# Half tiles, 64 side slots a batch and small operands in PSUM in the first block of a four-layer network

## The reference

```python
qkv = x @ w_qkv + b_qkv
qkv = conv2d(qkv, w_dw, groups=3 * c) + b_dw          # 3 x 3, one filter a channel
off = conv1x1(pconv(q_img, pconv_off_w[i]), w_off[i], b_off[i])
out = gather(y0, x0) * (1 - wy) * (1 - wx) + ...       # four corners a tap, at learned offsets
attn = softmax(einsum('bgnc,bgckn->bgnk', q * HC ** -0.5, keys), axis=-1)
out = einsum('bgnk,bgckn->bgnc', attn, values)
x = x + (out @ w_proj + b_proj)
```

## Time and profile before

| | us |
|---|---|
| median of three timed runs | 9134.66 |
| span of the profiled execution | 10539.2 |
| of it before the first gather | 313.0 |
| stretch of the tile loop, 313 to 7596 | 7283.0 |
| rest of the profiled span | 2943.0 |
| POOL busy in the tile loop | 4529.5 |
| DVE busy in the tile loop | 4016.5 |

### The profile page before, as it was taken

How to read it: one execution, slowest core, us unless ns; L and a number is a source line. 1 busy time by engine, 2 the same in 40 slices (tenths; PEclk the granted TensorE clock), 3 DMA queues, 4 the chain that set the end, 5 groups by cost and what they waited for, 6 DMA issues and landing times. The chain is left out here.

```text
span 10539.2 us, 107779 instructions
## 1 busy us (share of the span) xinstructions
PE 3679.2 (35%) x42500; PEld 2522.4 (24%) x42500; DVE 5657.8 (54%) x6593; ACT 1410.3 (13%) x2586; POOL 4585.7 (44%) x4748
## 2 busy tenths in 40 slices
PE   5103100012202211130121121000257478699997
PEld 3002000000201100020011011000134356588885
DVE  6275755556664455667455445544454355455554
ACT  1000000000000000000000000000012133244442
POOL 0565667765565556656555555777400000000000
PEclk7555555555555555555555555555567778899998
DMA  4432363323336233423632322333220633222224
GB/s 80 114 103 82 100 162 103 108 84 101 87 103 149 80 93 98 107 75 108 148 89 84 97 88 85 106 100 100 68 41 1 199 66 84 74 67 67 66 66 170
DMA packets 957938, 1001.43 MB, mean 95 GB/s; under 512 B 417257, under 2 KB 778578, under 8 KB 952914
## 3 DMA queue, kind: packets, MB, share of 16 engines
q0 software_dynamic: 221184, 604.27, 19.5%
q1 hardware_dynamic: 687234, 350.65, 13.9%
q10 hardware_dynamic: 49104, 40.35, 1.3%
HBM read 797.88 MB, written 190.61 MB: 94 GB/s over the span
## 5 line engine op out<-in xcount | busy, mean ns | idle before, releaser
L466 POOL DMA_INDIRECT l_rec<-records,l_row x4608 | 4529.5, 983 | 3003.4 <-issue 1526.7
L598 PE MATMUL l_pso<-l_id,l_att_t 128*128 128x128 f32 x128 | 60.2, 471 | 5183.5 <-DVE l_att_t L931 3100.6
L598 PEld LDWEIGHTS l_pso<-l_id,l_att_t 128*128 128x128 f32 x128 | 23.6, 185 | 5230.2 <-DVE l_att_t L931 3133.2
L916 DVE TENSOR_TENSOR l_rec<-l_rec,l_psv 128x4608 f32<-128x4608 f32 x128 | 634.0, 4953 | 1043.5 <-DMA l_rec<-records,l_row 991.1
L931 DVE TENSOR_REDUCE l_att_t<-l_rec 128x128 f32<-128x4608 f32 x128 | 1004.5, 7848 | 4.4
L2187 DVE COPY l3p_mix<-l3p_ps 128x512 f32<-128x512 f32 x1024 | 660.1, 686 | 572.8 <-PE l3p_ps L2063 572.8
L924 DVE TENSOR_REDUCE l_total<-l_prob 128x4 f32<-128x36 f32 x128 | 24.4, 191 | 1516.1 <-ACT l_prob L699 1489.1
L2149 ACT ACTIVATE l3p_mix<-l3p_ps 128x512 f32<-128x512 f32 x1024 | 556.7, 596 | 660.3 <-PE l3p_ps L2063 660.3
L929 DVE TENSOR_TENSOR l_rec<-l_rec,l_psv 128x4608 f32<-128x4608 f32 x128 | 634.0, 4953 | 4.4
L917 DVE TENSOR_REDUCE l_dots<-l_rec 128x144 f32<-128x4608 f32 x128 | 634.0, 4953 | 4.4
L2063 PE MATMUL l3p_ps<-l3p_psi,l3p_ms 32*128 32x128 f32 x16384 | 609.7, 283 | 19.4 <-DVE l3p_mix L2187 16.9
(11 more groups left out here) (357 smaller groups left out, 6994.1 us busy)
## 6 DMA issues: line engine op xcount, KB each, us to landing
l_rec<-records,l_row POOLq DMA_INDIRECT x4608
records<-l_area SPq DMA_DIRECT2D x96, 512.0 KB
l2b_w<-l_w SPq DMA_DIRECT2D x32, 1024.0 KB, 11.6
l_row<-meta SPq DMA_DIRECT2D x128, 154.0 KB
records<-l_rec SPq DMA_DIRECT2D x32, 512.0 KB
l_x_hat<-l3a_xout ACTq DMA_DIRECT2D x32, 512.0 KB, 3.6
l3p_xin<-l_x_hat SPq DMA_DIRECT2D x128, 128.0 KB, 3.1
l_y_raw<-l3p_yr SPq DMA_DIRECT2D x64, 256.0 KB, 3.5
```

What stands on the lines that cost most here:

```text
L466: pool.indirect_dma_start(out=rec[s % 2][:, k, :], out_offset=None, in_=records[b].rearrange("o g y x c d -> (o g y x) (c d)"), in_offset= ...
L598: pe.transpose(ps_a, att_t[:, :], id_s[:, :]).then_inc(s_att, 1)
L916: step(dve.tensor_tensor(keys, keys, asked.broadcast_to([P, GROUPS, TAPS * CORNERS, HC]), ALU.mult))
```

## The change

A tile is now handled in two halves of 18 gathers, two groups each. `rec` becomes a ring of four half buffers of the same total size; POOL may begin half h of tile t when DVE has summed half h of tile t - 2. DVE runs 12 steps on each half; the copy of the query into PSUM, before on ACT (L692), is DVE's first step of a tile. The residual of tile t is added in the second half of tile t + 1, after its scores; PE turns a tile at the end of its iteration and projects it at the start of the next; ACT copies it after the next exponential. `next(side)` is called twice a tile, and the jobs are dealt out over 40 slots for `points` (19 gaps before) and 24 for `linear` (11 before). The three small DMAs that shift images for the offset convolution go from ACT's queue to SP's for batches 1 to 3. `dots`, maxima, totals and shares move from SBUF to PSUM bank `psv`, so that each small DVE instruction has at most one input in SBUF. The arithmetic is the same.

```diff
+    RING, HT, HG = 4, GT // 2, GROUPS // 2
-        rec = [st.sb(f"rec{i}", [P, GT, REC]) for i in range(2)]
+        rec = st.sb("rec", [P, RING, HT, REC])
-        dots = st.sb("dots", [P, GT, CORNERS])
-        peak = st.sb("peak", [P, GROUPS])
-        total = st.sb("total", [P, GROUPS])
+        att_t = [st.sb(f"att_t{i}", [P, C]) for i in range(2)]
+        dots = ps_v[:, at_w:at_w + HT * CORNERS].rearrange("p (k c) -> p k c", c=CORNERS)
+        share = ps_v[:, at_s:at_s + HT]
+        peak, total = ps_v[:, at_s + HT:at_s + HT + HG], ps_v[:, at_s + HT + HG:at_s + HT + 2 * HG]
...
-        opening = [("qkv", (f, g), 1) for f in range(3) for g in range(NG)]
+        opening = [("qkv", (f, g), 5 + f) for f in range(3) for g in range(NG)]
-        lj += [("qv", g, 1 if g < 3 else 2 if g < 8 else 3 if g < 13 else 4) for g in range(2 * NG)]
+        lj += [("qv", g, 7 + g // 4) for g in range(2 * NG)]
...
@@ sync
+                    if slot == 15 and b:
+                        sp.wait_ge(a_dw, b * 3 + 1)
+                        shift(sp)
...
                 if t >= 3:
+                    next(side)
                     next(side)
@@ gpsimd
+                        hold(pool, s_row[s], 16 * i + 16, s_gate[1])
+                        for h in range(2):
+                            hold(pool, s_dve, AHEAD * STEPS * (i - 1) + summed(s + 2, h), s_gate[1])
+                            half(b, s, h)
@@ tensor
             for t in range(TILES):
-                pe.wait_ge(s_dve, t * STEPS + SUMMED)
-                pe.transpose(ps_a, att_t[:, :], id_s[:, :]).then_inc(s_att, 1)
-                pe.wait_ge(s_attc, t + 1)
-                pe.matmul(ps_p, att_c[:, :], wo0_s[:, :], start=True, stop=False)
-                pe.matmul(ps_p, ones[:, :], bo0_s[:, :], start=False, stop=True).then_inc(s_proj, 1)
+                if t:
+                    project(t - 1)
                 next(side)
+                next(side)
+                pe.wait_ge(s_dve, summed(t, 1))
+                pe.transpose(ps_a, att_t[t % 2][:, :], id_s[:, :]).then_inc(s_att, 1)
@@ scalar
+                for h in range(2):
+                    act.wait_ge(s_dve, scored(t, h))
+                    act.activation(prob[:, :], score[:, :], ACT.Exp).then_inc(s_exp, 1)
+                    if h == 0 and t >= 1:
+                        turned(t - 1)
+                    if h == 0 and t >= 2:
+                        store(t - 2)
+                    next(side)
@@ vector
+                    for f, at in ((0, 7), (1, 15), (2, 29)):
+                        if b and at <= slot < at + NG:
+                            g = slot - at
+                            filtered(f, g, img[f])
...
+                for h in range(2):
+                    if h == 0:
+                        step(dve.tensor_copy(ps_q, row[s][:, QUERY:META]))
+                    dve.wait_ge(s_rec[r], 16 * HT * (t // 2 + 1))
...
+                    if h == 1 and t >= 1:
+                        add(t - 1, step)
```

More of the change, by code:

```diff
@@ L244, in first_layers @@
         s_res = [st.sem(f"res{i}") for i in range(2)]
-        s_rec = [st.sem(f"rec{i}") for i in range(2)]
+        s_rec = [st.sem(f"rec{i}") for i in range(RING)]
         s_done = [st.sem(f"done{i}") for i in range(2)]
-        s_query = st.sem("query")
         s_exp = st.sem("exp")
@@ L278, in first_layers @@
         s_gate = st.gates()
-        STEPS, SCORED, SUMMED = 13, 6, 12
+        STEPS = 26
         TILES = BATCH * NT
@@ L321, in sides @@
                     for _ in linear(b - 1):
-                        gaps += 1
+                        slots += 1
                         yield
-                for _ in range(gaps, NT):
+                assert slots <= 2 * NT
+                for _ in range(slots, 2 * NT):
                     yield
@@ L352, in points @@
-                for _ in range(6):
-                    yield
-                sp.wait_ge(a_act, b * PA + taken(plan(b), after(plan(b), "qt")))
-                sp.dma_start(meta[b:b + 1, :, :, QUERY:META].rearrange("o t p m -> (o p) t m"), qry).then_inc(a_qst, 16)
-                for _ in range(7):
-                    yield
-                if b == 0:
-                    sp.wait_ge(a_act, PA)
-                    for part in range(4):
-                        keep(b, part)
-                sp.wait_ge(a_meta, b + 1)
@@ L486, in points @@
                 done_act, done_offs, pj = b * PA, b * NG, plan(b)
-                for gap in range(PG):
+                for slot in range(PG):
+                    if slot == 2:
+                        pe.wait_ge(a_x, b * 80 + 80)
+                        pe.wait_ge(a_stat, b + 1)
+                        pe.matmul(ps_s[:, 0:2], gm_s[:, :], m2[:, :], start=True, stop=True).then_inc(a_gsum, 1)
+                    if slot == 4:
+                        pe.wait_ge(a_nm, b + 1)
+                        for i in range(3):
+                            mm = pe.matmul(ps_s[:, 2 + i:3 + i], wq_s[:, i * P:i * P + P], sc[:, 3:4], start=True, stop=True)
+                        mm.then_inc(a_bias, 1)
                     for n, (kind, at, own) in enumerate(pj):
-                        if own != gap:
+                        if own != slot:
                             continue
@@ L609, in points @@
                 pj = plan(b)
[L610 to L611 removed]
+                for slot in range(PG):
+                    if slot == 3:
                         act.wait_ge(a_var, b + 1)
                         act.activation(sc[:, 2:3], sc[:, 4:5], ACT.Sqrt).then_inc(a_std, 1)
[L614 to L619 removed]
+                    if slot == 15 and b == 0:
+                        act.wait_ge(a_dw, 1)
+                        shift(act)
+                    if slot == 25:
+                        act.wait_ge(a_point, b + 1)
+                        act.activation(off[:, :, 2 * GT:OFFS], off[:, :, 2 * GT:OFFS], ACT.Sigmoid).then_inc(a_sig, 1)
                     for n, (kind, at, own) in enumerate(pj):
[L621 removed]
+                        if own != slot or kind == "offs":
                             continue
```

614 lines of the change are left out of this document (325 added, 289 removed).

## The result

The change takes 9125.62 us (median of 20 runs, 9113.14 to 9143.52), the kernel before 9146.61 (20 runs). The ratio is 0.9979, 95% interval 0.9973 to 0.9986: 21 us less, inside the 0.3% that the forecast calls no change, where it had said 9065. The profiled execution of the change has a span of 9124.6 us, as long as the timed runs; that of the kernel before had 10539.2. The two traces on record are thus not to be compared line by line, and the first thing to find was why.

What follows compares the result with a forecast made beforehand. POOL's gathers were taken as the bound, 128 x 45.1 = 5773 us; with 313.0 before and 3004.9 after, 9091. From the median, 9134.7 - 60 (pauses) - 11 (end) = 9064, forecast as 9065, range 9000 to 9107.

Steps and rivals of the forecast that it cites:

- The bound: Tile loop: POOL's row of gathers bounds it, 36 in 45.1 us a tile, 5773 us for 128 tiles.
- The end: After the last gather: DVE has only half a tile left, 25.3 - 14.0 = 11 us saved.
- the 60 us: Tile loop: POOL's pauses from side work queued ahead of exponentials, 0 to 90 us in timed runs, taken as 60.
- the sum 9091: Whole kernel before: 313.0 before the loop, 5773 of unpaused gathers, 3004.9 after; 44 us under the median.
- the queue ahead of the exponential: ACT: 24 bank copies of the q, k, v product take 33 us, so DVE waits some 22 for the exponential.
- Rival 1: Tile loop: the 44 us are not pauses of POOL, only the end is saved; 9124, no change; chance 0.20.
- The reading that failed: Profile before: recording delays signals, so most of POOL's 1165 us of waits exist in the profiled execution alone.
- its last sentence on the profile: Profiled span: falls from 10539 by several hundred us, as slots and 51 us of slack hide late signals too.
- The rule weighed: Gathers beside L918, L921, L926: two SBUF inputs contend with GpSimd, the change leaves one; would give 8975; trace does not show it.
- Rival 3: Gathers beside small DVE instructions L918, L921, L926 get cheaper: 90 us off, 8975; chance 0.09.
- Rival 4: POOL: doubled clusters of small DVE instructions slow gathers, 2.4 us more a tile, about 9370; chance 0.16, mild forms included.
- Rival 2: Tile loop: the gather's 0.30 us pause is absent from timed runs, DVE's waits are real; about 8000; chance 0.07.

Runs made afterwards that it cites:

- before_again: The kernel before, unedited, run once more for a trace on a chip with prompt signals: 9128.25 us, profiled span 9121.7.
- small_sbuf_2: The change with softmax's sums, maximum, total and shares back in SBUF, prompt signals: 9131.3 us, 0.9989 of the kernel before.

## Why the prediction was wrong

**The bound** was right: 36 gathers at 1.25 us a tile, 14.0 us for DVE's half, nothing for the extra instructions, POOL's third wait and SP's queue. DVE's busy time in the loop rose from 3975.8 us in `before_again` to 4275.7, and none of it is seen in the loop's time. Removing gathers confirmed it at the forecast's price.

**The end** was right in its size: from the last gather to the last sum, 27.2 us before and 15.8 after, 11.4 saved. It hardly shows, because what follows it takes 2959 to 2998 us in the traces of both kernels at hand.

**The step that failed** is the 60 us "for pauses of POOL in timed runs". The 44 us between the sum 9091 and the median were real, but they were not pauses: in `before_again`, as long as the timed runs, POOL never waits for DVE over 0.3 us, and the loop's 5820 us stand 47 above the 5773 of the sum by slow gathers. Of its 56.5 us of excess 9.7 lie in the four gaps. Some 32 lie in tiles 12, 13, 44, 45, 76 and 77, and the change has 34 in tiles 13, 14, 45, 46, 77 and 78, beside the same 128x1152 instructions, which the change doesn't touch.

What was mis-sized is the queue ahead of the exponential, 22 us. In `before_again`, ACT's 24 copies of the q, k, v product (L629: shortest, median and longest in ns, first and last start), then DVE's waits for the exponential (us in total, times, longest):

```profile
L629 ACT ACTIVATE l_area<-l_ps,l_bn x24: 689/689/693, 1901.2 to 1922.7; 128x512 f32<-128x512 f32 x24
```

```profile
DVE l_total L924 <- ACT l_prob L699: 95.1, 128, 8.2
```

The copies take 21 to 22 us and not 33, since the 1.38 us a bank came from a trace with late signals, and DVE waits 7.9 us behind these and 8.2 at most in any tile. The slack was read rightly: POOL has 18.0 us in the median tile before (8.7 at the least) and 52 in the change, where 18 and 51 were forecast. A tile of 28.1 + 13.7 + 8 stays under 63, so there was nothing to win back. Rival 1 named it, at 9124, and 9125.62 came. That it fits to 2 us is in part luck: it has the end alone in it, and the 21 us hold more than that.

**The reading that failed** stands ahead of it: that the 1165 us exist only while recording. Two other chips took 10506 and 10526 us unprofiled. Its choice for the time held on prompt chips, though the queue's price came from the late trace; its last sentence on the profile rested on it, and what it said (several hundred us off) is true as a time of the chips with late signals: 382 and 392 us, 3.6 and 3.8%.

**The 21 us** come apart like this, by the traces with prompt signals: 11 at the end, about 5 before the first gather (315.7 and 313.0 against 308.7 and 308.8), and 12 of excess, 9.7 of them the gaps. The sum, 28, is above the 13 to 25 of the interval. One execution can't settle it: the steady interval itself is 1.250 us in some executions and 1.253 in others, some 15 us a loop in kernels that are the same (5820.5 and 5804 us for the change, 5819.9 before). Undoing the hand-over, the hand-over with the dealing, or the operands gave back 4 to 15 us each by the ratios, in intervals that meet the change's, so which part brought the 21 us is not shown.

**The rule weighed.** The Trainium skill, "SBUF — State Buffer", section "Who interferes with whom", has a DVE instruction with two SBUF inputs contend with a GpSimd instruction that reads SBUF. L971 and L972 above show it. The change's small instructions were the wrong place to look: gathers beside L918, L921 and L926 take 0.95 us on average in `before_again`, as alone, and only the one that multiplies corner weights with shares holds them, for 4.3 us in `small_sbuf_2` and 2 in `before_again`, not 90. Rival 3 (8975) fell with that. Rival 4 fell too: the excess with late signals is 221 us before and 212 to 220 after, with prompt ones 56.5 and 44 to 45, though clusters doubled. The gathers of 1.54 and 1.93 us belong to late signals. Rival 2 fell, since gathers pause 0.30 us in executions as long as the timed ones.

## What to carry to other kernels

Before a profile that is longer than the timed runs is explained by recording, run the kernel again elsewhere: two conditions of chips gave 9147 and 10506 us for one program, and a change can be worth 0.2% in one and 3.7% in the other. A queue's rate is read from a trace of the condition whose time is forecast: here 33 us of copies were 22. Where an engine in order is the bound, its slow instructions are found by their excess over the steady duration, grouped by what runs beside them; pauses and slow instructions look alike in a sum. Slack and finer hand-over are worth what the lateness they absorb is worth, and cost nothing that shows otherwise.

## What the runs showed of the hardware

- With prompt signals a gather on GpSimd (0.95 us, next one 0.30 later) beside a string of DVE instructions of 0.64 us and more that have all operands in SBUF gets in only between two of them, at the first gap at 1.25 us or later: 1.36, 1.51, 1.59 and 1.39 us apart beside strings 0.68, 0.755, 0.795 and 1.39 apart, and 2.1 to 2.5 beside instructions 2.25 apart. Beside instructions 1.22 apart this rule fails: two gathers were held, by 0.22 and 0.06 us, and then none.
- One SBUF input is enough for it in an instruction that takes 0.76 us for 1152 elements. Beside the reductions over 2304 elements in 2.56 and 4.0 us, also with one SBUF input, gathers keep 0.95 while signals are prompt; so they do beside 4.42 us with an operand in PSUM.
- With late signals PE's instructions start multiples of 0.70 us apart in the stretch shown, beside gathers, and an exponential comes up to 56 us late. DVE's and ACT's busy times and the granted clock are unchanged; gathers have 212 to 228 us of excess in a loop instead of 22 to 57.
